# From the last heads to the router: halves of tokens, mean and scale ahead of the deviation, shared down weights split elsewhere, products in a new order

## What is computed

```python
def _L0_ffn_ref(x, gate_w, up_w, up_b, gw, gb, down_w, down_b, sh_gate_w, sh_up_w, sh_down_w):
    h = x.reshape(-1, Dm)                                  # 4096 x 256
    scores = jax.nn.sigmoid(h @ gate_w.T)                  # 4096 x 16
    cap = math.ceil(T / E * TOP_K)                         # 512
    topk_score, topk_ids = jax.lax.top_k(scores.T, cap)
    xin = h[topk_ids]
    up = jnp.einsum('ecd,efd->ecf', xin, up_w) + up_b[:, None, :]
    g = jnp.einsum('ecd,efd->ecf', xin, gw) + gb[:, None, :]
    eo = jax.nn.silu(g) * up
    eo = jnp.einsum('ecf,edf->ecd', eo, down_w) + down_b[:, None, :]
    flat = (eo * topk_score[..., None]).reshape(-1, Dm)
    out = jnp.zeros_like(h).at[topk_ids.reshape(-1)].add(flat)
    shared = jax.nn.silu(x @ sh_gate_w.T) * (x @ sh_up_w.T)
    return out + shared @ sh_down_w.T

h = _layernorm(x) * (1 + ca) + sa
x = x + ga * attention(h)          # softmax(q k) v per head, causal, then Wout
h = _layernorm(x) * (1 + cb) + sb
x = x + gb * _L0_ffn_ref(h, ...)
```

## Time and profile before

| | |
|---|---|
| median of 3 runs | 1192.36 us (1189.97 to 1192.46) |
| the profiled execution's own time | 1199.97 us |
| its span | 1198.2 us |
| mean granted TensorE clock in it | 0.961 of full speed |
| PE busy | 1119.2 us (93% of the span) |
| DVE busy | 867.4 us (72%) |
| POOL busy | 633.1 us (53%) |
| ACT busy | 599.5 us (50%) |

### The profile page before, as it was taken

One profiled execution on the slowest core, in us unless ns is written; L12 is line 12 of the kernel. 1 busy time (PEld: TensorE's weight loads), 2 busy tenths in 40 slices (PEclk: granted clock), 3 DMA queues, 4 the chain that ended last, 5 costly groups with the idle time before them and its releaser, 6 DMA issues.

```text
span 1198.2 us, 21657 instructions
## 1 busy us (share of the span) xinstructions
PE 1119.2 (93%) x7463; PEld 870.1 (73%) x7464; DVE 867.4 (72%) x2208; ACT 599.5 (50%) x1085; POOL 633.1 (53%) x668
## 2 busy tenths in 40 slices
PE   8788989898988997999879999999999999999997
PEld 5345646555545565888768888888888888888886
DVE  5578788797977868887977776677766677767662
ACT  2247767776776644322224553444553444454441
POOL 4125376574665734222326565656566656666654
PEclk8779999998999998999989999999999999999999
DMA  7636667877668624767244556555556555455531
GB/s 194 84 57 121 106 121 172 146 152 168 129 149 167 177 97 172 234 193 219 63 150 122 153 129 164 129 127 127 146 133 159 129 137 122 144 146 143 134 84 18
DMA packets 100333, 165.44 MB, mean 138 GB/s; under 512 B 18424, under 2 KB 65016, under 8 KB 98176
## 3 DMA queue, kind: packets, MB, share of 16 engines
q1 hardware_dynamic: 83360, 137.04, 45.0%
q0 software_dynamic: 14336, 25.70, 11.2%
q10 hardware_dynamic: 2528, 1.32, 0.9%
HBM read 103.71 MB, written 34.11 MB: 115 GB/s over the span
## 4 chain that ended last, share of the span: by engine, by line
PE 57%; DVE 13%; DMA 8%; POOL 7%; issue 6%; ACT 3%; SPq 3%; ACTq 1%; DVEq 0%; POOLq 0%
PE MB L543 14%; PE LB L543 13%; PE LB L856 8%; PE MB L856 7%; DVE junk L1281 3%; POOL out_y L1877 3%; PE UB L672 3%; DMA HT<-Us 3%; PE LB L634 2%; PE UB L543 2%; PE XB L543 2%; SPq L327 2%; DMA rdD<-D 1%; DMA XT<-hD 1%; DMA DN<-rdD 1%
## 5 line engine op out<-in xcount | busy, mean ns | idle before, releaser
L1837 POOL TENSOR_TENSOR HTl<-HF,HTh 128x512 fp32r<-128x512 f32 x156 | 218.0, 1403 | 215.1 <-ACT HTh L1064 214.7
L1281 DVE CUSTOM_DVE_ANT_0 junk<-MB,MK 128x256 bf16<-128x256 f32 (+3 forms) x512 | 219.8, 484 | 67.7 <-PE MB L611 66.5
L1745 POOL TENSOR_SCALAR_AFFINE_SELECT P<-P 128x256 f32<-128x256 f32 x256 | 102.0, 422 | 157.8 <-ACT P L1004 157.8
L1877 POOL DMA_INDIRECT out_y<-EO,IDX x64 | 108.8, 1699 | 76.5 <-DVE EO L1706 66.4
L1075 ACT ACTIVATE SIL<-LB,gbT 128x512 f32<-128x512 f32 x64 | 44.0, 687 | 195.3 <-PE LB L543 190.1
L1002 ACT ACTIVATE P<-LB 128x768 f32<-128x768 f32 x128 | 103.9, 812 | 71.4 <-PE LB L634 71.1
L611 PE MATMUL MB<-KS,QS 48*128 48x256 f32 (+3 forms) x512 | 128.3, 364 | 11.0 <-DMA KS<-ST 5.2
L634 PE MATMUL LB<-QS,KS 50*128 50x256 f32 (+3 forms) x512 | 122.7, 357 | 15.0 <-ACT P L1002 12.2
L1064 ACT ACTIVATE HTh<-HF 128x512 fp32r<-128x512 f32 x156 | 98.0, 628 | 69.9 <-DVE HF L1626 69.8
L634 PEld LDWEIGHTS LB<-QS,KS 50*128 50x128 f32 x512 | 78.9, 191 | 63.5 <-issue 51.2
L856 PE MATMUL LB<-WDh,HTh 128*128 128x256 f32 x320 | 95.5, 299 | 8.5 <-DVE tb L1670 8.5
(11 more groups left out here) (298 smaller groups left out, 3042.7 us busy)
## 6 DMA issues: line engine op xcount, KB each, us to landing
WR<-in_gw SPq DMA_DIRECT2D x16, 1024.0 KB
WR<-in_uw SPq DMA_DIRECT2D x16, 1024.0 KB
WR<-in_dw SPq DMA_DIRECT2D x16, 1024.0 KB
QS<-ST SPq DMA_DIRECT2D x96, 128.0 KB, 4.7
KS<-ST SPq DMA_DIRECT2D x90, 128.0 KB, 5.6
hD<-h SPq DMA_DIRECT2D x8, 1024.0 KB, 5.2
XT<-hD SPq DMA_DIRECT2D x7, 1024.0 KB, 8.2
X<-in_x SPq DMA_DIRECT2D x8, 512.0 KB, 6.3
```

Of the source, the lines that this page charges most:

```text
L1281: m = e.tensor_tensor_reduce(junk[:, o:o + w], MB[:, o:o + w], MK[:, 512 - w:512], 1.0, -3e38, ALU.add, ALU.max, NM[:, k // 4, 4 * (k % 4) ...
L1745: m = e.affine_select(out=dd, in_=dd, compare_op=ALU.is_ge, fill=0.0, base=0, pattern=[[0, 2], [1, 128]], channel_multiplier=-1)
L1837: e.tensor_tensor(HTl[:, slot, :], hf_of(n)[:], HTh[:, slot, :].bitcast(F32), ALU.subtract).then_inc(g_ht, 1)
L1877: e.indirect_dma_start(out=out2, out_offset=bass.IndirectOffsetOnAxis(ap=IDX[x_ % 3][:, q:q + 1], axis=0), in_=EO[:, q, :], in_offset=None ...
```

## The change

Nothing that is computed changes. What the parts do:

- **Halves.** The sums of the last unit are inverted in halves of the tokens (64x256). Those of group 0 go between the copies of `raw(3)`, `raw(4)` and `raw(5)` in head 6 of the last unit, those of group 1 stand with `normalise(i)` and `split_heads(i)` for each half, behind five products of the shared MLP. ACT's part is `split_last(i)`, and the first `outproj` waits for the first half alone.
- **Mean and scale ahead of the deviation.** `last_h2` on DVE takes the place of `scale2` (ACT), `shift2` (DVE) and of the second POOL instruction in `moments`: `th = (X - mean) * scale` in four instructions of 128x256 needs no deviation, then `H2 = th * rs2 + shift` in four more.
- **Down weights.** They are loaded during head 3 of the last unit into a tile of their own, `SDR` (where a batch of `X` was), ACT makes the high part right behind its last exponential, and POOL the low part. The two `cut(1, ...)` on ACT and DVE go, and the numbering of pieces shifts.
- **Order.** DVE's and ACT's entries `w` 0 to 9 are written out by hand: `outproj` is followed at once by `last_h2`, and the products of the shared MLP come before and after. On ACT two SiLU stand before the copy of the last heads. On PE `scores` of batch 6 goes to LB ahead of `outproj` and is carried to DVE by an ACT copy `SC6`, `h2T` of batch 7 goes from `w = 10` to `w = 8`, `scores` of batch 7 into the product of `w = 8`. `W_TOPK`, `W_PIECES` and `W_INDEX` are one less.
- **DMA queue.** On SP the store of `X` (batch 6) and of `H2` (batch 6) go ahead of the last heads' DMAs; `load_xl(0)` and the load of batch 2 wait until these have landed.

The core of the diff:

```diff
-W_TOPK = 11
+W_TOPK = 10
 W_LOAD = 13
-W_PIECES = 40
-W_INDEX = 41
+W_PIECES = 39
+W_INDEX = 40
...
+    SDR = at("SDR", 33664, [128, 4, D])
+    SC6 = at("SC6", 50048, [128, 512])
...
+                if (u, k) == (NU - 1, 3):
+
+                    e.wait_ge(c_xd, 16 * (NB - 2))
+                    e.wait_ge(a_th, 2 * (NB - 2))
+                    e.dma_start(SDR[:], kn(sd)).then_inc(c_sd, 16)
+                if (u, k) == (NU - 1, 6):
+                    store_x2(NB - 2)
...
+        store_h2(NB - 2)
         take_heads(NU - 1, 1)
-
         e.wait_ge(p_pv, 2 * NU)
-        e.dma_start(WR[1][:, 0:1024].rearrange("p (k n) -> p k n", k=4), kn(sd)).then_inc(c_wr[1], 16)
         e.wait_ge(a_p, 2 * 8 * NU)
+        e.wait_ge(c_us[1], 32 * NU)
         load_xl(0)
...
             if w == 6:
+
+                o = 112 - 16 * (NB - 2)
+                e.wait_ge(d_h2, 2 * (NB - 2) + 2)
+                terms3(LB[:, 1024:1536], lambda k: GPh[:, k, o:o + 128], lambda k: GPl[:, k, o:o + 128],
+                       lambda k: h2[:, 0, k, :], lambda k: h2[:, 1, k, :]).then_inc(p_sc, 1)
                 outproj(NB - 1, 0, "o1")
                 outproj(NB - 1, 1, "o0")
-            if w == 7:
-                scores(NB - 2, "s1")
-            if w == 10:
+            if w == 8:
                 h2T(NB - 1, 0, "h0")
                 h2T(NB - 1, 1, "h1")
...
-                    for r in {2: (0,), 3: (1,), 5: (2,), 6: (3, 4)}.get(k, ()):
+                    for r in {2: (0,), 3: (1,), 5: (2,)}.get(k, ()):
                         raw(r)
+                    if k == 6:
+                        raw(3)
+                        last_inverses(0, 0)
+                        raw(4)
+                        last_inverses(0, 1)
...
+        def last_h2():
+
+            settled()
+            for k in range(4):
+                m = e.bn_aggr(mv2[:, k, :], st2[:, k, :])
+            kept(m)
+            settled()
+            e.wait_ge(a_th, 2 * (NB - 1))
+            e.tensor_scalar(rs2[:], mv2[:, :, 1], EPS, None, ALU.add).then_inc(d_mv2, 1)
+            b = NB - 1
+            for k in range(4):
+                m = e.scalar_tensor_tensor(out=th[:, k, :], in0=X[:, b % 4, k, :], scalar=mv2[:, k, 0:1],
+                                           in1=BT[b % 2][:, 2, :], op0=ALU.subtract, op1=ALU.mult)
+            kept(m)
+            settled()
...
+            e.wait_ge(g_rs2, NB)
+            for k in range(4):
+                m = e.scalar_tensor_tensor(out=H2[:, k, :], in0=th[:, k, :], scalar=rs2[:, k:k + 1],
+                                           in1=BT[b % 2][:, 1, :], op0=ALU.mult, op1=ALU.add)
+            m.then_inc(g_h2, 2)
```

More of the change, by code:

```diff
@@ new lines, in vector_program @@
+        h2T(NB - 2, 0, "h0")
+        h2T(NB - 2, 1, "h1")
+        shared_glu(0, 3)
+        shared_glu(1, 0)
+        last_inverses(1, 0)
+        normalise(0)
+        last_inverses(1, 1)
+        split_heads(0)
+        normalise(1)
+        split_heads(1)
+        for j in range(2):
+            outproj(NB - 1, j, f"o{1 - j}")
+            add_x(NB - 1, j)
+        stats2(NB - 1, 0)
+        stats2(NB - 1, 1)
+        last_h2()
+        shared_glu(1, 1)
+        shared_glu(1, 2)
+        h2T(NB - 1, 0, "h0")
@@ new lines, in vector_program @@
+        h2T(NB - 1, 1, "h1")
+        e.wait_ge(a_sc6, 1)
+        e.wait_ge(d_lg, NB - 2)
+        e.tensor_tensor(LG[:], LG[:], SC6[:], ALU.add).then_inc(d_lg, 1)
+        shared_down(0, 0)
+        scores(NB - 1, "s0")
+        shared_down(0, 1)
+        topk_step(0)
+        topk_step(T_BIT)
+        shared_glu(1, 3)
+        shared_down(0, 2)
+        shared_down(0, 3)
+        ticks[0] = -2
+        for w, (kind, b, i) in enumerate(ORDER):
+            if w < W_TOPK:
+                continue
```

174 lines of the change are left out of this document (89 added, 85 removed).

## The result

| | before | changed |
|---|---|---|
| median of 20 runs each, in turns | 1196.36 us (1189.97 to 1201.99) | 1192.03 us (1185.19 to 1201.0) |
| the profiled execution's own time, span | 1199.97, 1198.2 us | 1189.41, 1187.7 us |
| PE, DVE busy | 1119.2, 867.4 us | 1115.0, 865.0 us |

The changed kernel takes 0.9966 of the time before, 95% interval 0.995 to 0.9983: faster, by 4.1 us (2.0 to 6.0). The three runs shown ahead of the prediction had a median of 1192.36; with 17 more of the same kernel it is 1196.36. The difference forecast was 4.4.

A forecast was written before the change was run, and what follows sets the result against it. PE was taken to bound the kernel, except where it idles or runs at half clock: 12.1 us lost between attention and search would become 7.7. The 4.4 gained, off the median 1192.36, gave 1188.0 us; range over all 1184.5 to 1193.0.

The forecast's parts named there:

- Term 1: Group 0's half reciprocals among attention's copies: PE waits at raw(6), attention ends 1.9 us later (ends 0 and +2.5).
- Term 2: Last heads on DVE: PE waits 3.0 us instead of 3.31 ahead of the last projection, clock staying up.
- the halves win nothing: In term 2: splitting the last heads' steps gains nothing, as 1.67 us of reciprocal precedes HNl either way.
- Term 3: From last projection to h2T of batch 7: PE waits 0.9 us (0.7 to 2) instead of 5.21 plus clock loss.
- Term 4: Waits for scores of batch 7 and the sigmoid: 0.4 us (about 0.27 before) and 0.3 us (1.11 before).
- Term 5: EO of batch 0 behind the sigmoid delays the reload of GBt and XL of batch 1: +1.0 us (0 to +2.5).
- Rival B: First reload of XL takes 14.03 us as one load did, holding DVE and PE: 1196.4 us; chance 0.12.
- Term 6: ACT's queue before Us, table load included, fits in 4.28 us of idle: 0; with the skill's drain 0.9 worse.
- Term 7: End of ORDER, search one entry earlier: 0 (ends -2.9 and +1), since the last batch's store and reload set it.
- Sum: PE's lost time from attention's end to the search: 12.1 us before, 7.7 after, gain 4.4 us.
- rival C: DVE's load from 560 to 612 us sets the end of ORDER, which shortens by 2.9: 1185.1 us; chance 0.13.
- Rival A: POOL meetings delay the last heads: PE waits 5.0 us and keeps the 1.9 clock loss: 1191.9 us; chance 0.20.

The follow-up runs named there:

- recip_back: Changed kernel with group 0's half reciprocals behind the last copy of the first products again; 0.9958 of the time before.
- scores_thrice: Changed kernel with the six products of the scores of batch 6 made three times, filling PE's idle ahead of the last projection; 0.9955 of before.
- whole_heads: Changed kernel with group 1's reciprocals, quotients, high and low parts each in one piece of 512 tokens; 0.9974 of before.
- deviation_first: Changed kernel with the last batch normalised as before the change (power and product on POOL, scalings on ACT); 0.9995 of before.
- products_ahead: Changed kernel with two MLP products on DVE between the last batch's statistics and its moments; 0.9986 of before.
- down_on_dve: heads_first with the low part of the down weights subtracted on DVE ahead of tf instead of on POOL; 0.9964 of before.
- combo: Changed kernel with the edits of recip_back, heads_first and scores_thrice together; 0.9965 of before.
- combo_later: combo with the search one entry of ORDER later; 0.9975 of before.
- combo_earlier: combo with the search one entry of ORDER earlier; 0.9967 of before.
- search_later: Changed kernel with the search and what hangs on it one entry of ORDER later, as before the change; 0.9993 of before.
- heads_first: Changed kernel with the last heads' reciprocals, halves and low parts on DVE ahead of the fourth and fifth MLP product; 0.9943 of before.
- before_filled: Kernel before the change, with eighteen products in PE's idle ahead of the scores of batch 6; 0.9979 of before.
- heads_reload: heads_first with the last two outputs of batch 0 on DVE ahead of the search's first count; 0.9963 of before.
- recip_thrice: Changed kernel with the edits of recip_back and scores_thrice, the two products left ahead of the last heads; 0.9958 of before.
- the four of combo: combo, combo_later, combo_earlier, and combo with batch 0's last two outputs on DVE ahead of the search's first count (the last 0.997 of before).

## Why the prediction was right and wrong

The difference, its sign and most of its terms held; the absolute time did not, and that one term hit to 0.1 us and the sum to 0.4 is in part luck. The steps that failed are two: the level from which the difference was taken, and the clock behind the projection.

- **Term 1, +1.9: +1.4.** The last value product ends 23.24 us into the stretch instead of 21.82. The `HT` load took 2.8 us from issue (431.48) to landing (434.30) where I took the 3.45 of the other one, and the reciprocal and copy behind it came 0.6 us sooner. recip_back showed what I had not priced: behind `raw(7)` the same 3.5 us cost 0.9, so the term is net 0.6.
- **Term 2, wait 3.0: 3.01,** and the projection 11.3 us after the last value product: 11.3. Three errors stand beside that. "No longer than the 3.31 after which the clock stayed up" is the step of the mechanism that failed: 3.01 dropped the clock and cost 1.2 (scores_thrice). I read one spared wait as a rule. And "the halves win nothing" is worth 1.2 us (whole_heads), which my sum had used unawares, since the 4.1 us that it put from the reciprocal to the low part are the halves'. And the hit is partly luck: "about +6.6" is +7.2 by its own terms (2.7, three at 0.6, two at 1.36), which would have made a wait of 3.6. Only one of the two meetings with POOL counted, so the reciprocal did start at +6.8; from it to the end of the low part it took 4.5 us, with no meeting, where I had 4.1 and 0.65 for one.
- **Term 3, about +9.5 and a wait of 0.9: +11.3 and 1.12.** 1.5 of the difference is the half clock (the projection took 4.44 us instead of 2.98). Its parts, measured: mean and scale ahead of the deviation 2.1 and up to 3.25 with the clock (deviation_first), products out of the way 1.1 (products_ahead), down weights off DVE 1.4 (down_on_dve).
- **Term 4, 0.4 and 0.3: 0.27 and 0.** The sigmoid hid wholly.
- **Term 5, +1.0: 0.63 on PE,** 0.75 on DVE (I gave it 1 to 3). By the chain of waits `XL` landed 5.87 us after its issue (482.65), near the 5.6 used, and DVE went on 0.74 later (489.26), which is 13.7 us after PE's last `down` of batch 0 (475.5); I had 13.5, though the 6 and 5.6 that I named make 11.6. Rival B, 14 us, did not come.
- **Term 6, 0: 0.** By the Trainium skill ("ScalarE: Activation LUTs", What ACT_TABLE_LOAD costs) about 1.38 us of drain would have made `Us` late; the changed trace again shows no drain: the instruction ahead ended at 441.22, the load ran from 441.24 for 1.28 us, and SiLU began at 442.53.
- **Term 7, 0: 0** by combo, combo_later and combo_earlier, whose stretches agree within 0.4 us; rival C is not borne out there. Search_later, the one test on the changed kernel itself, does not exclude it. The 1.2 us by which the profile's end looks shorter (131.5 us from the transposes of `S` to the experts, against 130.0 and an entry of 2.7) fit the clock: between 560 us and the experts it was at half for 10.2 us instead of 13.7. The 2 us by which I called C ("shorter by more than 2 us") are not reached.
- **Sum.** 1.4 + 0.2 + 3.0 + 1.5 + 1.1 + 0.3 + 0.6 = 8.1 instead of 7.7, so a gain of 4.0 out of 12.1; measured 4.1. That 8.1 is near 7.7 is luck: the clock and the wait for `h2T` cost 1.7 more than forecast, terms 1, 4 and 5 cost 1.3 less. The two profiles say about the same: from the projection of batch 6 to the transposes of `S` 65.44 and 57.80 us, 7.6 less, of which 2.7 are the entry that moved behind; 4.9 are left, in single executions. Rival A was half true: not the wait of 5.0 but its clock loss came, behind a wait of 3.0. Its rule, "SBUF — State Buffer", Who interferes with whom, in the Trainium skill, agrees with the trace (`RW` 1.69 and 1.27 us beside POOL's `WDl` and `HNl`, 0.69 alone). The meeting of 1.27 fell ahead of 1.26 us in which DVE waited for ACT anyway and cost nothing; behind the one of 1.69 DVE had no idle time up to the reciprocal, so its 1.0 us lies in the wait of 3.0.
- **The level.** "I take the difference to the median 1192.36" is the step that failed and made the time wrong: 1188.0 against 1192.03. That median stood 4.0 us below the one of 20 runs. The traces show how uncertain three runs are: the projection of batch 6, ahead of which the kernels differ by that one load alone, starts anywhere from 418.0 (combo) to 429.0 us (whole_heads).

## What to carry to other kernels

When a reorder shortens a chain, price each part beside the others, not alone: two products that were free behind a slow projection cost 1.2 us as soon as the projection was fast. A wait that once left the clock up is no bound for another; give such a drop a chance and a price (here 1.2 us) instead of zero. Take the level of a forecast from as many runs as the spread asks for: three runs of a kernel whose executions differ by 10 us put it 4.0 us too low. And read single profiles by a stretch with the same work in it, split into work, idle and time at half clock, and trust that split no further than the work column repeats.

## What the runs showed of the hardware that was not expected

The length of an idle of PE does not decide alone whether the granted clock falls to half. Ahead of the projection of batch 7 it fell behind (or late in) idles of 2.31 us (heads_first), 3.00 to 3.02 (changed, products_ahead, deviation_first, search_later), 3.44 (before_filled), 3.88 (recip_back) and 4.20 (whole_heads), and it stayed up behind 2.31 (heads_reload), 3.31 (before), 1.11, 0.44 and 0.24 (recip_thrice, combo, scores_thrice). In down_on_dve 1.75 us were enough, the clock falling 1.2 us into the projection. Ahead of `h2T` it fell behind 2.59 to 2.61 us in five kernels (the four of combo and heads_reload) and behind 3.24 (deviation_first), and stayed up behind 2.95 in down_on_dve and 2.18 in products_ahead. The cleanest case is one wait late in the search, which all kernels have:

```profile
560.96 0.38 PE L817 MATMUL XB<-PT,C 128*128 128x1 f32 x2 [2.36 <-DVE PT L1603]
```

In sixteen of the seventeen profiles it lasts 2.35 to 2.38 us; the clock fell behind it (or in it) in ten, among them before and changed, and stayed up in six (heads_first, deviation_first, combo, combo_later, before_filled, heads_reload). The same wait ahead of the same instruction can go either way. The time at half clock in one stretch of 190 us varied from 6.8 to 23.9 us over the kernels here, and half of that difference, some 8 us, is time. A reciprocal takes its time by the columns and not by the partitions: 64x256 1.74 us, 64x512 and 128x512 3.35 us, where a product of 128x512 takes 0.69.
